# Attention and FFN kernel: the FFN one tile at a time with keys as rows, and the DMAs of the probabilities issued by ScalarE

## The reference

```
x   : 2 x 2048 x 512      ctx : 2 x 77 x 384       8 heads of 128
h   = layernorm(x)
sim = (h Wq)(ctx Wk)^T * 128^-0.5 ; sim = (sim - mean) * 1.5 + mean
x   = x + softmax(sim) (ctx Wv) Wout + bout        # all 154 keys for every row
h   = layernorm(x);  hp = h shifted by one row (0 at the start of a batch)
xr  = mu_r*h + (1-mu_r)*hp ;  xk = mu_k*h + (1-mu_k)*hp
r   = sigmoid(xr Wr^T) ;  k = relu(xk Wk^T)^2
out = x + r * (k Wv^T)                             # Wr, Wk, Wv are 512 x 512
```

## Time and profile before

| | us |
|---|---|
| median of 3 runs | 744.74 (743.87 to 744.83) |
| the profiled execution | 744.54 |
| its span on the core | 742.7 |
| PE busy in the span | 736.4 |
| DVE busy | 516.0 |
| ACT busy | 426.8 |
| POOL busy | 123.7 |

### The profile page before, as it was taken

The page is one execution under the profiler, slowest core; times in us unless marked ns, Lnnn a source line. Parts: engine busy times, 40 slices in busy tenths (PEclk is TensorE's granted clock), DMA queues, the critical chain, the costliest instruction groups (busy, mean ns, idle before and its releaser), DMA issues.

```text
span 742.7 us, 13556 instructions
## 1 busy us (share of the span) xinstructions
PE 736.4 (99%) x3948; PEld 643.0 (87%) x3948; DVE 516.0 (69%) x1085; ACT 426.8 (57%) x1204; POOL 123.7 (17%) x279
## 2 busy tenths in 40 slices
PE   9999999999999999999999999999999999999998
PEld 8957888888988888898888889888888988888887
DVE  3678987777667766666776766677666667766662
ACT  3568865575746556564655656465665646565332
POOL 1111111202121120212112021211202121120211
PEclk9999999999999999999999999999999999999999
DMA  9966643545444353545435354543535454343301
GB/s 330 252 152 172 202 136 115 148 147 177 140 146 147 117 164 87 176 142 167 129 109 159 93 175 144 163 126 115 167 84 175 143 167 128 109 156 93 112 28 43
DMA packets 87239, 106.52 MB, mean 143 GB/s; under 512 B 9999, under 2 KB 64169, under 8 KB 87211
## 3 DMA queue, kind: packets, MB, share of 16 engines
q1 hardware_dynamic: 87172, 106.15, 47.6%
q10 hardware_dynamic: 39, 0.04, 0.0%
HBM read 58.70 MB, written 47.45 MB: 143 GB/s over the span
## 4 chain that ended last, share of the span: by engine, by line
PE 90%; SPq 5%; DVE 1%; DMA 1%; ACT 1%; issue 1%; POOL 0%; POOLq 0%; DVEq 0%
PE ffn L494 12%; PE ffn L496 12%; PE ffn L495 12%; PE scores L495 9%; PE scores L496 9%; PE scores L494 9%; PE attended L496 9%; PE attended L495 9%; PE attended L494 9%; SPq L353 3%; SPq L336 1%; PE attended L544 1%; PE attended L543 1%; DMA x_rows<-normed 1%; SPq L333 1%
## 5 line engine op out<-in xcount | busy, mean ns | idle before, releaser
L494 PE MATMUL scores<-A_hi,xT_hi 128*128 128x462 f32 x372 | 129.9, 349 | 0.8 <-DVE B_lo L973 0.8
L495 PE MATMUL scores<-A_lo,xT_hi 128*128 128x462 f32 x372 | 130.4, 351 | 0.0
L496 PE MATMUL scores<-A_hi,xT_lo 128*128 128x462 f32 x372 | 130.0, 349 | 0.0
L775 ACT ACTIVATE probs<-scores,neg_max 128x154 f32<-128x154 f32 x248 | 93.2, 387 | 46.7 <-DVE neg_max L1033 46.6
L496 PE MATMUL attended<-B_hi,pT_lo 128*128 128x512 f32 x288 | 112.5, 391 | 0.0
L495 PE MATMUL attended<-B_lo,pT_hi 128*128 128x512 f32 x288 | 112.4, 390 | 0.0
L494 PE MATMUL attended<-B_hi,pT_hi 128*128 128x512 f32 x288 | 112.1, 389 | 0.0
L1033 DVE TENSOR_REDUCE neg_max<-scores 128x3 f32<-128x462 f32 (+1 forms) x93 | 53.3, 581 | 80.9 <-PE scores L496 80.9
L1334 POOL TENSOR_SCALAR var<-stats 128x1 f32<-128x1 f32 x64 | 13.2, 206 | 462.4 <-DVE stats L979 461.3
L494 PEld LDWEIGHTS scores<-A_hi,xT_hi 128*128 128x128 f32 x372 | 70.2, 189 | 8.0 <-issue 1.7
L495 PEld LDWEIGHTS scores<-A_lo,xT_hi 128*128 128x128 f32 x372 | 70.1, 188 | 5.6
(11 more groups left out here) (171 smaller groups left out, 1583.3 us busy)
## 6 DMA issues: line engine op xcount, KB each, us to landing
prob_rows<-probs SPq DMA_DIRECT2D x32, 704.0 KB, 4.1
probs_handed<-prob_rows SPq DMA_DIRECT2D x128, 176.0 KB, 3.4
x_rows<-normed SPq DMA_DIRECT2D x61, 256.0 KB, 2.4
handed<-x_rows SPq DMA_DIRECT2D x244, 64.0 KB, 1.9
x_in<-in_x SPq DMA_DIRECT2D x32, 256.0 KB, 3.0
out<-x SPq DMA_DIRECT2D x31, 256.0 KB, 3.7
wq<-in_L_xattn_Wq SPq DMA_DIRECT2D x2, 1024.0 KB, 10.6
wout<-in_L_xattn_Wout SPq DMA_DIRECT2D x1, 2048.0 KB, 20.1
```

The costliest lines, as they stand in the source:

```text
L494: te.matmul(psum, left[0], right[0], start=first, stop=False)
L495: te.matmul(psum, left[0], right[1], start=False, stop=False)
L496: return te.matmul(psum, left[1], right[0], start=False, stop=last)
L775: last = nc.scalar.activation(probs[:, q, cols], score_banks(t)[b][:, (h - h0) * J:(h - h0 + 1) * J], ACT.Exp, bias=neg_max[:, h:h + 1], a ...
```

## The change

The FFN works on one tile per step: `key_rows(t-1)`, `gate_rows(t-1)`, `value_rows(t-2)`. Keys have the mixed columns stationary and 512 weight columns moving, and come out as rows in bank T[1]. The squares must then be turned: ACT writes `act`, SP stores it and hands it back (`store_squares`, `hand_squares`, a new DRAM tensor), DVE turns it (`squares_turn`), ACT and DVE split it. The second norm gets a landing buffer of its own, `handed2`. `add_x(t)` stands ahead of `x_turn(t+3)` on DVE. `store_probs` and `hand_probs` move from SP's stream to ACT's. All written orders at the start are new, and so are those of the last three tiles. Shortened, with the orders at the start cut to what the prediction speaks of:

```diff
+        handed2 = sb("handed2", [P, D])
+                 "v": sb("raw_wv", [P, 4 * DC, P], at=at_ffn_weights)}
@@ SP, step @@
-                if is_tile(t + 2):
-                    store_probs(t + 2)
                 if is_tile(t) and not is_last(t):
                     store_x2(t)
+                if is_tile(t - 1) and not is_last(t - 1):
+                    store_squares(t - 1)
                 if is_tile(t) and not is_last(t):
                     hand_x2(t)
-                if is_tile(t + 2):
-                    hand_probs(t + 2)
+                if is_tile(t - 1) and not is_last(t - 1):
+                    hand_squares(t - 1)
@@ PE @@
-            def key_columns(q):
...
+            def key_rows(t):
+                if begun(t - 1):
+                    te.wait_ge(relu_ready, t)
+                else:
+                    te.wait_ge(W_ready, DC)
+                te.wait_ge(mixed_split["k"], t + 1)
+                ffn_rows(T[1], (mixed_hi["k"], mixed_lo["k"]), WT["k"]).then_inc(k_done, 1)
@@ PE, step @@
                 if is_tile(t):
                     attend(t)
+                if is_last(t):
+                    value_rows(t - 3)
+                key_rows(t - 1)
+                gate_rows(t - 1, turn_last_x2 if is_last(t) else None)
+                if is_last(t - 1):
+                    turn_last_squares()
+                if not is_last(t + 1):
+                    value_rows(t - 2)
+                if is_last(t - 1):
+                    last_value_rows()
@@ PE, start @@
             scores(3)
             attend(1)
+            scores(4)
+            attend(2)
+            key_rows(0)
+            gate_rows(0)
+            scores(5)
+            key_rows(1)
+            gate_rows(1)
+            attend(3)
+            value_rows(0)
+            key_rows(2)
+            gate_rows(2)
+            value_rows(1)
             turns(te, step)
@@ ACT @@
+            def store_probs(t):
+                act_e.wait_ge(probs_ready, t + 1)
+                nc.scalar.dma_start(p_dram[bass.ds(t * P, P), :], probs[:].rearrange("p q k -> p (q k)")
+                             ).then_inc(probs_stored, 16)
+            def hand_probs(t):
+                act_e.wait_ge(probs_stored, 16 * (t + 1))
+                act_e.nop(nofuse=True)
+                if begun(t - 1):
+                    act_e.wait_ge(probs_turned, t)
...
+                for q in range(4):
+                    nc.scalar.dma_start(probs_handed[q * Q:(q + 1) * Q, :, :], rows[q]).then_inc(probs_landed, 16)
@@ ACT, step (new order) @@
+                hand_probs(t + 1); x_norm(t + 3); exponentials(t + 2, 0); mixed_high("k", t - 1)
+                exponentials(t + 2, 1); squares_hi(t - 2); mixed_high("r", t - 1); exponentials(t + 2, 2)
+                normalise_early(t + 2); pack_hi(t + 2); x_hi(t + 3); store_probs(t + 2); x2_norm(t)
+                squares(t - 1); probs_hi(t + 1); open_gate(t - 1)
@@ ACT, start @@
             x_norm(3, 3)
+            act_e.wait_ge(consts_ready, 1)
+            store_probs(0)
             for b in range(2):
                 values_hi(2 * b)
                 values_hi(2 * b + 1)
                 exponentials(1, b)
+                if b == 0:
+                    hand_probs(0)
...
             x_norm(4, None)
+            store_probs(1)
             weights_hi("k")
             x_hi(3)
             for b in range(3):
                 exponentials(2, b)
+                if b == 0:
+                    hand_probs(1)
             normalise_early(2)
             pack_hi(2)
             weights_hi("r")
+            store_probs(2)
...
             for b in range(3):
                 exponentials(3, b)
+                if b == 0:
+                    hand_probs(2)
             x_hi(4)
@@ DVE @@
+            def squares_turn(t):
+                dve.wait_ge(act_landed, 64 * (t + 1))
+                if begun(t - 1):
+                    dve.wait_ge(kv_done, t)
+                turn_blocks(actT[:], act_handed[:], DC).then_inc(act_turned, 1)
@@ DVE, step (new order) @@
+                x_statistics(t + 3); open_values(t - 3); maxima(t + 2, 0); x2_turn(t - 1); mix_change(t - 1)
+                mix("k", t - 1); maxima(t + 2, 1); squares_turn(t - 2); mix("r", t - 1); maxima(t + 2, 2)
+                inverse_early(t + 2); mixed_low("k", t - 1); squares_lo(t - 2); mixed_low("r", t - 1)
+                normalise_late(t + 2); pack_lo(t + 2); add_x(t); x_turn(t + 3); probs_turn(t + 1)
+                x_lo(t + 3); probs_lo(t + 1)
@@ DVE, start (new order from tile 2 on) @@
+            mixed_low("k", 0); mixed_low("r", 0); inverse_early(4); x_turn(5); normalise_late(4); x_lo(5)
+            x2_turn(1); pack_lo(4); mix_change(1); add_x(2, 0, 2); probs_turn(3); mix("k", 1)
+            x_statistics(6, 2, 2); probs_lo(3); mixed_low("k", 1); mix("r", 1)
```

More of the change, by code:

```diff
@@ L476, in _ @@
             load_x(4, 0)
-            store_probs(3)
+            hand_x(5)
             load_x(5, 1)
@@ L855, in step @@
             def step(g, s):
-                t, q, half = place(g, s)
-                if is_pair(q) and half == 1:
-                    squares(q, 1)
-                    squares_hi(q)
+                t = place(g, s)
+                if is_tile(t + 1):
+                    hand_probs(t + 1)
                 if comes_in_steps(t + 3):
@@ L946, in _ @@
             pack_hi(3)
+            store_probs(3)
             weights_hi("v")
@@ L1169, in step @@
             def step(g, s):
-                t, q, half = place(g, s)
-                pair = q if half == 0 else q + 1
+                t = place(g, s)
                 if comes_in_steps(t + 3):
                     x_statistics(t + 3, (s + 3) % 4, g + (s + 3) // 4 + 1)
-                if half == 0 and is_pair(q - 1) and not is_last(t - 1):
-                    open_values(q - 1, 1)
-                if is_pair(q) and half == 1:
-                    squares_lo(q)
+                ends = is_last(t) or is_last(t - 1)
@@ L1178, in step @@
+                if not ends:
+                    open_values(t - 3, (s + 1) % 2)
                 if is_tile(t + 2):
-                    for b in range(3):
-                        maxima(t + 2, b)
-                    inverse_early(t + 2)
-                if is_tile(t - 1):
-                    x2_turn(t - 1, 1 - half, pair)
-                    mix_change(t - 1, 1 - half, pair)
-                    for w in "kr":
-                        mix(w, t - 1, 1 - half, pair)
+                    maxima(t + 2, 0)
@@ new lines, in step @@
+                x2_turn(t - 1)
+                mix_change(t - 1)
+                mix("k", t - 1)
+                if ends:
+                    mixed_low("k", t - 1)
+                if is_last(t):
+                    add_x(t, g, s)
+                if is_tile(t + 2):
+                    maxima(t + 2, 1)
+                if not ends:
+                    squares_turn(t - 2)
+                mix("r", t - 1)
+                if is_tile(t + 2):
+                    maxima(t + 2, 2)
+                    inverse_early(t + 2)
@@ L1302, in _ @@
             for w in "kr":
-                mixed_low(w, 0, 0)
-            x2_turn(1, 1, 0)
-            mix_change(1, 1, 0)
-            mix("k", 1, 1, 0)
+                mixed_low(w, 0)
             inverse_early(4)
-            mixed_low("k", 1, 1)
-            add_x(2, 0, 2)
-            normalise_late(4)
-            x_turn(5)
-            mix("r", 1, 1, 0)
-            x_lo(5)
-            mixed_low("r", 1, 1)
-            pack_lo(4)
+            x_turn(5)
+            normalise_late(4)
+            x_lo(5)
+            x2_turn(1)
+            pack_lo(4)
+            mix_change(1)
+            add_x(2, 0, 2)
             probs_turn(3)
+            mix("k", 1)
+            x_statistics(6, 2, 2)
             for i in range(3):
                 probs_lo(3, i)
-            weights_lo("v")
-            turns(dve, step, from_second=True)
+            mixed_low("k", 1)
+            mix("r", 1)
+            maxima(5, 0)
+            mixed_low("r", 1)
+            maxima(5, 1)
+            squares_turn(0)
+            maxima(5, 2)
+            weights_lo("v", range(0, 2))
+            x2_turn(2)
+            inverse_early(5)
+            squares_lo(0)
+            weights_lo("v", range(2, 4))
+            mix_change(2)
+            normalise_late(5)
+            mix("k", 2)
+            x_turn(6)
+            mixed_low("k", 2)
+            pack_lo(5)
+            x_lo(6)
+            mix("r", 2)
+            mixed_low("r", 2)
+            squares_turn(1)
+            add_x(3, 0, 3)
+            squares_lo(1)
+            probs_turn(4)
+            open_values(0, 0)
+            for i in range(3):
+                probs_lo(4, i)
+            turns(dve, step)
             last_rows()
```

454 lines of the change are left out of this document (231 added, 223 removed).

## The result

The changed kernel takes 752.27 us (median of 6, 750.55 to 753.35), the kernel before 744.79 (6 runs, 743.03 to 745.71): ratio 1.0106, interval 1.0094 to 1.0117. It is slower, by 7.5 us where I predicted 2. The profiled execution took 753.35 us, the longest of the six and 1.1 over their median.

A forecast was written before the change was run, and what follows sets the result against it. PE was taken as the bound, busy for 736.4 of 742.7 us. The terms -5.0 + 0 + 6.0 + 1.3 = +2.3 us on the profiled 744.54 gave 746.8 us, range 740.6 to 751.0.

The forecast's parts named there:

- Term 1: PE's work: 24 key matmuls of 512 columns per pair replace 48 of 256, saving 5.0 us in all.
- Term 2: The loop's steps: every operand is ready before PE wants it, so no cost, 0 us.
- Term 3: The start: each hand_probs sits between exponentials that DVE and PE wait for, costing 6.0 us (sum 6.05).
- Term 4: The end: attend(31) waits 1.3 us, squares turned on PE add 0.5, old waits of 0.5 go; +1.3 us.
- Rival 1: Start hides more than counted, stalls there only 1 to 2.5 us, time 740.5 to 742.0; chance 0.28 with wider band.
- Rival 4: No stall at all, time 739.6 us; chance 0.05.
- Rival 2: DMA issues on ACT cost 0.66 us each, time 750.0 us; chance 0.10.
- Rival 3: A wait in the loop, xT_lo first, paid in 25 steps; 1 us gives 772 us; chance 0.07.

The follow-up runs named there:

- run 1: Changed kernel with the stores and reads of the probabilities issued by SyncE again; 744.27 us, ratio 0.9999 to the kernel before.
- run 4: Changed kernel with the probabilities' reads moved behind the first exponentials in ScalarE's step (step 30: behind the keys' high part); 747.51 us, ratio 1.0057.
- run 5: Changed kernel with open_values(0) first on DVE, x_root(6) ahead of keep_halo(1) on POOL, and the probabilities' reads later on ScalarE; 744.41 us, ratio 1.0004.
- run 9: Changed kernel with open_values(0) first, all maxima and first sums' inverse ahead of x2_turn, all exponentials and early products ahead of the keys' high part; 750.06 us.
- run 3: Changed kernel with x_root(6) ahead of keep_halo(1) on POOL at the start; 750.80 us, ratio 1.0094.
- run 8: Changed kernel with the third maxima ahead of squares_turn and mix r on DVE; 763.33 us, ratio 1.0252.
- run 6: Changed kernel with matmuls nobody reads added on PE, 8 ahead of value_rows(1) and 14 ahead of key_rows(29); 752.41 us.
- run 10: Kernel before with one part of the change alone: store and reads of the probabilities issued by ScalarE; 745.73 us, ratio 1.0018.

## Why the prediction was wrong

The sign was right, the size wrong: 7.5 us measured, 2 predicted, and the time outside my range. The profiled execution is 6.6 us over my 746.8. By the prediction's own terms scores(6) starts at 139.95 and 68.0 us remain behind scores(31); it was 141.49 and 72.4, so 1.5 of the miss lie at the start, 0.7 in the loop and 4.4 at the end.

- **Term 1, -5.0: right.** Key matmuls follow at 0.227 us, the step is 21.48, and in run 1 the 25 steps take 537.0 us where the kernel before takes 541.3. (A pair of steps takes 43.3 us before; the stretch of 42.6 that I called a pair is a little short.) Run 1 shows the rest of the account: with the queue undone the change is worth nothing, so the 5.0 us are spent on waits of the start and the end.
- **Term 2, the loop: the step that failed.** I took x2's trip, from its store's issue to its turn, as 5.7 us, with a landing of 1.9 from the earlier trace rows. That row is of a kernel with one queue, where the same queue issued the probabilities' reads behind those of x2. I even had both times in hand, x2's reads until 1.7 of the step and `hand_probs` at 20.6 of the step before, and gave their meeting no price. The trip took 8.5 us (419.97 to 428.50), `xk_lo` was ready at 12.7 of the step shown instead of 9.1, and the slack of 4.2 was 0.6. And I counted each operand against PE only. That a late x2 delays `pack_lo`, `add_x` and so the next x2 was not looked for, since I never followed what stands behind x2_turn on its engine around to x2_turn. The loop itself lost only 0.7 us, but it takes back what the start gains and hands step 30 a late x2. Runs 4, 5 and 9 showed it.
- **Term 3, the start, +6.05: size nearly right, reasons mostly wrong, so that the nearness is partly luck.** In place of my 6.05, scores(6) came 7.6 us after the 133.9 without stalls. The first place was right: from the first exponential of tile 1 to the last `B_hi` ScalarE takes 6.35 us before and 8.13 now, so `hand_probs(0)` put 1.8 us into it as I had said, and scores(2) came 0.99 us later for my 1.15. In the four runs with SyncE's queue that stretch takes 6.4 us, in ten of the eleven with ScalarE's 7.9 to 8.3 and in one 6.9. Of the other places, attend(1), scores(4) and attend(2) had no wait to speak of. ScalarE's queue issues beside activations that are already under way: four reads of 1.8 us held the exponentials back by 0.6 (tile 2) and 0.8 us (tile 4), not 1.83. key_rows(1) and gate_rows(1) bore what was left of that; run 1 has 1.6 us back up to there. gate_rows(1)'s other part was POOL's order (run 3), and value_rows(1), which I had not named, waited for DVE behind the squares' reads. These met the store of tile 5's probabilities (reads at 126.07, store at 126.40), but they met it just so in runs 4 and 8, where DVE waited 1.1 us for them instead of 2.5; why they took longer here is open.
- **Term 4, the end, +1.3: mis-sized, it measured 5.7.** key_rows(29), not attend(31), waited, 3.7 us with what came before the first matmul, and then ran 1.7 us longer at the half clock; the cause is Term 2's late x2. With the reads apart (run 4) the end is 2.9 us shorter and attend(31) waits 2.2, so attend(31)'s wait was of the right kind, behind another.
- **The clock was missing from the sum.** 1.7 us in each of two stages. In run 6, without it, the median was no different, within the bounds given there.
- **The Trainium skill**, page "DMA: Bandwidth & Descriptors", section "Issuing engines are not separate DMA queues", says that DMAs issued by ScalarE, SyncE or GpSimd run on the same 16 DMA engines and interleave. I used it to say that the second queue brings nothing, and stopped there. The runs fit the rule and show another side of it: reads that run beside others land later, 2.6 us for 1.9.
- **The rivals.** Rivals 1 and 4 needed stalls of less than 5.0 us at the ends; there were more. Rival 2 gave 750.0, near the time, by issues of 0.66 us; their median was 0.36, so its reason is out. Rival 3 (a wait in the loop, paid 25 times) didn't come in this kernel, but in run 8: 0.38 us a step, for `xk_lo`, not for `xT_lo`.

Not settled: why scores(2) and value_rows(1) swing by 1.4 to 2 us between executions of the same code (at scores(2) it is the first exponential of tile 1 that swings, from 48.67 to 50.43), and of the 1.4 us of run 10, which part is issuing and which is the swing: its stretch up to the last `B_hi` is 1.8 us longer than before, but began 0.9 sooner. That x2's reads are late because the probabilities' reads take the same engines' time is the likeliest reading of runs 1 and 4, but no run measured it by itself.

## What to carry to other kernels

When a transfer moves to another queue, lay its new time of issue over those of all others that land just in time: one queue had kept them apart. Look for rings besides the path through the bound engine: from each wait for a DMA follow the instructions behind it, on all in-order engines, and see whether they lead back to that DMA's own input. A chain that ended last with 10% on an engine that is 98% busy was the sign of such a ring here (78 to 83% in runs 1, 4, 5 and 9, where it was open), and a gain that is given back in the loop was another.

## What was new in the hardware's behaviour

- ScalarE's queue issued DMAs, mostly in 0.32 to 0.48 us each, while its activations ran, but not freely: at tiles 1, 2 and 4 three exponentials ran beside the four issues, and the next instruction started within 0.05 us of the end of the last issue. So four reads held ScalarE up by 0.6 us at tile 2, 0.8 at tile 4 and 1.7 at tile 1, where one issue took 1.41 us. The view puts the 1.66 us of tile 1 down to PE, but the product that this copy reads had ended by 48.5 us. The timeline of ACT in the changed kernel:

```profile
49.32 0.39 ACT L793 ACTIVATE probs<-ffn,neg_max 128x154 f32<-128x154 f32 x1 [1.02 <-DMA prob_rows<-probs]
49.38 0.34 ACTq L783 DMA_DIRECT2D probs_handed<-prob_rows  x1
50.25 1.41 ACTq L783 DMA_DIRECT2D probs_handed<-prob_rows  x1
51.69 0.48 ACTq L783 DMA_DIRECT2D probs_handed<-prob_rows  x1
52.20 0.59 ACT L864 CAST B_hi<-scores 128x512 fp32r<-128x512 f32 x1 [1.66 <-PE scores L633]
...
69.73 0.45 ACTq L783 DMA_DIRECT2D probs_handed<-prob_rows  x1
70.23 0.39 ACT L793 ACTIVATE probs<-scores,neg_max 128x154 f32<-128x154 f32 x1 [0.58 <-issue]
```

- Reads of 64 KB landed 1.8 to 2.0 us after issue in x2's last trip of run 4, and 4.2 to 4.5 us after it in that of the changed kernel, beside 704 KB issued by ScalarE (3.3 to 4.7 us in the step shown above).
- PE's clock fell to 1.2 GHz behind waits of 1.81 us (value_rows(1)) and 3.53 us (key_rows(29)) of the changed kernel, but not behind another of 1.81 us in the same trace, at gate_rows(1), nor behind 1.78 (run 1) and 2.23 us (run 4) at attend(31), where it was granted 1.00 for the whole stage. So the length of one wait doesn't tell it. The stretch of gate_rows(1), columns as above:

```profile
117.55:120.35 2.80, 2.80 (x13) 2.33 (x13) 2.80 (x6) 2.61 (x13) 0.00 (x0) 1.00 0.26 79
```
